# Block normalizations of the experts, keys and feed-forward stages: one fp32 product per statistic, after an addition of the two channel halves on VectorE

## What is computed

```python
def _layernorm(x, axis=-1, eps=1e-05):
    m = jnp.mean(x, axis=axis, keepdims=True)
    v = jnp.var(x, axis=axis, keepdims=True)
    return (x - m) / jnp.sqrt(v + eps)
...
h = _layernorm(x, axis=-1) * (1 + cb) + sb
x = x + gb * _L0_ffn_ref(h, L0_ffn_w_router, L0_ffn_w_gate, L0_ffn_w_down)
...
h = _layernorm(x, axis=-1) * (1 + ca) + sa
x = x + ga * _L1_attn_ref(h, L1_attn_Wq, L1_attn_Wk, L1_attn_Wphi, L1_attn_Wy_w, L1_attn_Wy_b, L1_attn_We_w, L1_attn_We_b)
...
h = _layernorm(x, axis=-1) * (1 + cb) + sb
x = x + gb * _L1_ffn_ref(h, L1_ffn_w1_w, L1_ffn_w1_s, L1_ffn_w2_w, L1_ffn_w2_s, L1_ffn_h1_w, L1_ffn_h1_s, L1_ffn_h2_w, L1_ffn_h2_s, L1_ffn_w3_w, L1_ffn_w3_s)
```

## Time and profile before

| | |
|---|---|
| median of 3 runs (lowest to highest) | 4892.88 us (4888.24 to 4893.66) |
| the profiled execution | 4881.97 us |
| its span | 4880.3 us |
| PE busy | 4384.0 us (90%) |
| DVE (VectorE) busy | 3936.3 us (81%) |
| ACT (ScalarE) busy | 3422.2 us (70%) |
| POOL (GpSimd) busy | 3121.2 us (64%) |
| stage B, from the span's start | 811 to 975 us |
| stage K | 1076 to 1193 us |
| stage R | 4167 to 4880 us |

### The profile page before, as it was taken

How to read it: one execution, slowest core, us unless ns; L and a number is a source line. 1 busy time by engine, 2 the same in 40 slices (tenths; PEclk the granted TensorE clock), 3 DMA queues, 4 the chain that set the end, 5 groups by cost and what they waited for, 6 DMA issues and landing times.

```text
span 4880.3 us, 84137 instructions
## 1 busy us (share of the span) xinstructions
PE 4384.0 (90%) x28586; PEld 2320.3 (48%) x28586; DVE 3936.3 (81%) x6598; ACT 3422.2 (70%) x2401; POOL 3121.2 (64%) x2716
## 2 busy tenths in 40 slices
PE   7888876888899999999999999999999998899998
PEld 3333333475344444444444444444444444677777
DVE  2889786625899999999999999999999999322225
ACT  2223221322999999999999999999999998444443
POOL 1576572532777777777777777777777776243334
PEclk8888777889999999999999999999999999999999
DMA  6000001353000000000000000000000001100002
GB/s 224 0 0 1 0 0 40 119 182 135 1 5 2 2 4 2 17 4 2 2 4 2 17 4 2 2 4 2 11 5 3 3 5 36 71 18 9 17 26 87
DMA packets 70909, 131.01 MB, mean 27 GB/s; under 512 B 8279, under 2 KB 46647, under 8 KB 66160
## 3 DMA queue, kind: packets, MB, share of 16 engines
q1 hardware_dynamic: 61552, 106.21, 6.4%
q0 software_dynamic: 9216, 23.17, 1.3%
HBM read 74.66 MB, written 61.03 MB: 28 GB/s over the span
## 4 chain that ended last, share of the span: by engine, by line
DVE 36%; PE 19%; issue 18%; ACT 6%; POOL 4%; DVEq 1%; POOLq 1%; DMA 0%; another core or an unknown queue 0%; ACTq 0%; SPq 0%
DVE e_slots L811 23%; PE banks L2318 11%; DVE e_slots L768 5%; ACT e_slots L599 2%; DVE ew L811 2%; POOL e_slots L695 2%; PE banks L465 1%; PE banks L1667 1%; POOL e_slots L701 1%; DVE half_max L775 1%; ACT L620 1%; ACT e_slots L590 1%; PE banks L1721 1%; ACT L603 1%; PE banks L506 1%
## 5 line engine op out<-in xcount | busy, mean ns | idle before, releaser
L811 DVE CUSTOM_DVE_ANT_0 e_slots<-e_slots,banks 128x1024 f32<-128x1024 f32 x2048 | 2389.6, 1216 | 41.6 <-PE banks L506 34.3
L599 ACT ACTIVATE e_slots<-e_slots 128x4096 f32<-128x4096 f32 x512 | 1851.8, 3624 | 89.8 <-POOL e_slots L701 65.5
L506 PE MATMUL banks<-ex_parts,sel 128*128 128x512 f32 x4096 | 1481.2, 448 | 175.1 <-DVE ew L811 127.6
L695 POOL TENSOR_SCALAR e_slots<-k,qt 128x1024 f32<-128x1024 f32 x889 | 988.3, 1121 | 587.5 <-DVE e_slots L768 509.5
L465 PE MATMUL banks<-e_slots,w_score 128*32 128x256 f32 x16384 | 1186.9, 391 | 77.4 <-ACT e_slots L599 76.2
L506 PEld LDWEIGHTS banks<-ex_parts,sel 128*128 128x128 f32 x4096 | 633.6, 189 | 894.4 <-DVE ew L811 750.4
L701 POOL TENSOR_SCALAR e_slots<-e_slots,qt 128x1024 f32<-128x1024 f32 x889 | 987.2, 1122 | 51.2 <-POOL e_slots L695 25.5
L465 PEld LDWEIGHTS banks<-e_slots,w_score 128*32 128x32 f32 x16384 | 392.6, 109 | 719.2 <-issue 401.2
L590 ACT ACTIVATE e_slots<-k,qt 128x1024 f32<-128x1024 f32 x508 | 564.6, 1135 | 1.5 <-DVE ew L811 1.4
L2448 POOL TENSOR_TENSOR g_l<-tmp,g_h 128x512 fp32r<-128x512 f32 x192 | 260.4, 1356 | 420.1 <-ACT g_h L2415 288.2
L768 DVE TENSOR_SCALAR e_slots<-k,qt 128x1024 f32<-128x1024 f32 x635 | 431.9, 748 | 0.0
(11 more groups left out here) (360 smaller groups left out, 4907.2 us busy)
## 6 DMA issues: line engine op xcount, KB each, us to landing
stage<-in_h SPq DMA_DIRECT2D x16, 1024.0 KB, 4.9
moe_slots<-empty_slot SPq DMA_DIRECT2D x1, 10320.0 KB, 38.2
slots<-moe_slots SPq DMA_DIRECT2D x8, 1290.0 KB
moe_out<-empty_slot SPq DMA_DIRECT2D x1, 8192.0 KB, 59.0
two_rows<-moe_out SPq DMA_DIRECT2D x16, 512.0 KB, 6.0
stage<-in_w SPq DMA_DIRECT2D x6, 1024.0 KB, 6.6
w_down<-in_w_down SPq DMA_DIRECT2D x1, 4096.0 KB, 12.2
x_between<-x_tokens SPq DMA_DIRECT2D x8, 512.0 KB, 3.7
```

The source lines that it names most:

```text
L506: ins = nc.tensor.matmul(spread[n % 2][:, half * W:(half + 1) * W], c_["sel"][:, half, n, :], ex_parts[:, par, :], start=True, stop=True)
L599: nc.scalar.activation(e_slots[:, par, four, :], e_slots[:, par, four, :], ACT.Sqrt, bias=EPS_RHO).then_inc(sqrt_done, 1)
L695: nc.gpsimd.tensor_scalar(e_slots[:, par, n, :], k2[:, :], FLT_MAX, qt[:, par, 1, place(n):place(n) + 1], ALU.min, ALU.max).then_inc(z_cla ...
L811: nc.vector.tensor_tensor_reduce(out=e, in0=e, in1=spread[n % 2], scale=1.0, scalar=0.0, op0=ALU.mult, op1=ALU.add, accum_out=ew[:, q, pla ...
```

## The change

In the stages B, K and R (all blocks of R but the first, whose normalization is made in stage C) VectorE adds the two channel halves of the tokens into a buffer of 128 x 512 (`b_sum`, `k_sum`, and in stage R the no longer used `empty_slot`), and the two halves of the squares in place. PE then makes one product where it made two. Two new semaphores, `halves_summed` and `squares_summed`, tell PE. The wait for the loaded tokens goes from PE's `mean` to VectorE's new `summed`, which in stage R is the first thing in VectorE's `ffn`. The stages A and C are as before.

```diff
@@ -213,7 +213,7 @@
...
                      ("taken", [P, E], fp32), ("taken_now", [P, E], fp32), ("row", [P, BT], fp32),
...
-                     ("expert", [P, E], fp32), ("out_row", [P, NTT], fp32), ("ln_even", [P, 6 * W], fp32)] + LN_BUFFERS("b2"))
+                     ("expert", [P, E], fp32), ("out_row", [P, NTT], fp32), ("b_sum", [P, 2, W], fp32), ("ln_even", [P, 6 * W], fp32)] + LN_BUFFERS("b2"))
         b_ |= phase([("slots", [P, N_SLOTS, SPP, SLOT_W], fp32), ("hid_t", [P, 3, HC, P], fp32),
...
                      ("first", [P, SPP], fp32), ("second", [P, SPP], fp32), ("w_first", [P, SPP], fp32),
@@ -225,7 +225,7 @@
                       ("cvec", [P, CC], fp32), ("cdiag", [P, CC, P], fp32), ("crow", [P, C], fp32),
                       ("k_sd", [P, W // P], fp32), ("k_rs", [P, W // P], fp32),
...
-                      ("v_out", [P, 2, W // P * C], fp32), ("k_cent", [P, 2, CC, W], fp32), ("k_sq", [P, CC, W], fp32)])
+                      ("v_out", [P, 2, W // P * C], fp32), ("k_cent", [P, 2, CC, W], fp32), ("k_sq", [P, CC, W], fp32), ("k_sum", [P, W], fp32)])
         b_base.close()
         x_layer0.close()
...
@@ -264,6 +264,7 @@
         mod_loaded, mod_tanh, mod_silu, first_mm, mod1_loaded, mod1_mm = (sem(s) for s in (
             "mod_loaded", "mod_tanh", "mod_silu", "first_mm", "mod1_loaded", "mod1_mm"))
         consts_ready = sem("consts_ready")
+        halves_summed, squares_summed = sem("halves_summed"), sem("squares_summed")
         lnm, lnc, lns, lnv, lnd, lno = (sem(s) for s in (
             "ln_mean", "ln_centered", "ln_squared", "ln_var", "ln_std_done", "ln_out"))
 
@@ -402,6 +403,7 @@
...
 
         LN_R = ln_first["R"]
+        r_sum = empty_slot[:, 0:W]
 
         N_C_LOADS = 6
 
@@ -1585,12 +1587,15 @@
             first = ln_first["B"]
 
             def mean(i):
-                ln_pe_mean(pe, first + i, x_of(i))
+                pe.wait_ge(halves_summed, i + 1)
+                pe.wait_ge(lnc, first + i + 1)
+                nc.tensor.matmul(bank(6), ones_mean[:, :], b_["b_sum"][:, i % 2, :], start=True, stop=True).then_inc(lnm, 1)
 
             def var(i):
 
                 pe.wait_ge(lnd, first + i)
-                ln_pe_var(pe, ln_b[i % 2], first + i)
+                pe.wait_ge(squares_summed, i + 1)
+                nc.tensor.matmul(bank(7), ones_mean[:, :], ln_b[i % 2][1][:, 0, :], start=True, stop=True).then_inc(lnv, 1)
 
             def router(i):
                 pe.wait_ge(lno, first + i + 2)
@@ -1691,17 +1696,17 @@
                 ins.then_inc(out_mm_b, 1)
 
             def k_mean(i):
-                pe.wait_ge(x_moe, i + 1)
-                ln_pe_mean(pe, LN_K + i, x_of(i))
+                pe.wait_ge(halves_summed, NBLK + i + 1)
+                pe.wait_ge(lnc, LN_K + i + 1)
+                nc.tensor.matmul(bank(6), ones_mean[:, :], k_ph["k_sum"][:, :], start=True, stop=True).then_inc(lnm, 1)
 
 
             def k_var(i):
-                pe.wait_ge(lns, LN_K + i + 1)
+                pe.wait_ge(squares_summed, NBLK + i + 1)
                 pe.wait_ge(lno, LN_K + i + 1)
                 for t in range(TPB):
-                    for k in range(CC):
-                        ins = nc.tensor.matmul(banks[:, 7, t:t + 1], k_ph["k_sq"][:, k, t * P:(t + 1) * P], ones_mean[:, 0:1],
-                                               start=k == 0, stop=k == CC - 1, skip_group_check=True)
+                    ins = nc.tensor.matmul(banks[:, 7, t:t + 1], k_ph["k_sq"][:, 0, t * P:(t + 1) * P], ones_mean[:, 0:1],
+                                           start=True, stop=True, skip_group_check=True)
                 ins.then_inc(lnv, 1)
 
             def spread_root(i):
@@ -1864,6 +1869,15 @@
                 dve.wait_ge(lnm, first + i + 1)
                 nc.vector.tensor_tensor(ln_b[i % 2][0][:, :, :], X[:, :, i * W:(i + 1) * W],
...
+
+            def summed(i):
+                nc.vector.tensor_tensor(b_["b_sum"][:, i % 2, :], X[:, 0, i * W:(i + 1) * W], X[:, 1, i * W:(i + 1) * W],
+                                        ALU.add).then_inc(halves_summed, 1)
+
+            def squares(i):
+                sq = ln_b[i % 2][1]
+                dve.wait_ge(lns, first + i + 1)
+                nc.vector.tensor_tensor(sq[:, 0, :], sq[:, 0, :], sq[:, 1, :], ALU.add).then_inc(squares_summed, 1)
 
             def normed(i):
                 b = i // BPB
@@ -1947,18 +1961,26 @@
...
                 nc.vector.tensor_copy(b_["slot_of"][:, b, :, :], packed[:, 3:5, :]).then_inc(rows_ready, 1)
 
+            summed(0)
+            summed(1)
             centred(0)
             centred(1)
+            squares(0)
+            squares(1)
+            summed(2)
             normed(0)
             normed(1)
             logits(0)
             dve.wait_ge(lno, first + 1 + 1)
             centred(2)
             logits(1)
+            squares(2)
             less_max(1)
             dve.wait_ge(cum_read, 1)
             choose(0)
             for i in range(NBLK):
+                if i + 3 < NBLK:
+                    summed(i + 3)
                 if i + 2 < NBLK:
                     normed(i + 2)
                 if i:
@@ -1970,6 +1992,8 @@
                 if i % BPB == 0:
                     place_rows(i // BPB)
                 silu(i, 1)
+                if i + 3 < NBLK:
+                    squares(i + 3)
                 if i + 2 < NBLK:
                     logits(i + 2)
                     if (i + 2) % BPB == BPB - 1:
@@ -2020,6 +2044,16 @@
...
                                                          x, ALU.mult, ALU.add)
                 ins.then_inc(x_moe, 1)
+                dve.wait_ge(x_moe, i + 1)
+                if i:
+                    dve.wait_ge(lnm, LN_K + i)
+                nc.vector.tensor_tensor(k_ph["k_sum"][:, :], X[:, 0, i * W:(i + 1) * W], X[:, 1, i * W:(i + 1) * W],
+                                        ALU.add).then_inc(halves_summed, 1)
+
+            def k_squared(i):
+                sq = k_ph["k_sq"]
+                dve.wait_ge(lns, LN_K + i + 1)
+                nc.vector.tensor_tensor(sq[:, 0, :], sq[:, 0, :], sq[:, 1, :], ALU.add).then_inc(squares_summed, 1)
 
             def k_centred(i):
                 dve.wait_ge(lnm, LN_K + i + 1)
@@ -2106,6 +2140,7 @@
             add(0)
             k_centred(0)
             add(1)
+            k_squared(0)
             k_rooted(0)
             k_centred(1)
             k_normed(0)
@@ -2113,6 +2148,8 @@
                 queries(i)
                 if i == NBLK - 1:
                     row_masks()
+                if i + 1 < NBLK:
+                    k_squared(i + 1)
                 if i + 2 < NBLK:
                     add(i + 2)
                 if i + 1 < NBLK:
@@ -2306,7 +2343,6 @@
             end_phase(sp, ph["R"])
 
         def pe_r(pe):
-            bufs = [w_["r_cent"], w_["r_sq"], w_["r_std"], w_["r_std"]]
...
 
             def product(dst, w, o, hi, lo, n_k, ready=None):
@@ -2321,8 +2357,13 @@
 
             def mean(b, h):
                 n = ln_first_r(b * BPB + h)
-                pe.wait_ge(xr_loaded[h], b * 16 + 16)
-                ln_pe_mean(pe, n, w_["xr"][:, h, :, :])
+                pe.wait_ge(halves_summed, b * BPB + (2 * NBLK + h))
+                pe.wait_ge(lnc, n + 1)
+                nc.tensor.matmul(bank(6), ones_mean[:, :], r_sum, start=True, stop=True).then_inc(lnm, 1)
+
+            def var(b, h):
+                pe.wait_ge(squares_summed, b * BPB + (2 * NBLK + h))
+                nc.tensor.matmul(bank(7), ones_mean[:, :], w_["r_sq"][:, 0, :], start=True, stop=True).then_inc(lnv, 1)
 
             def ffn(b, h, nxt):
                 i = b * BPB + h
@@ -2346,7 +2387,7 @@
                         pe.wait_ge(hi_done, i * PARTS + (OC + o - 1))
...
                 if nxt:
-                    ln_pe_var(pe, bufs, ln_first_r(nxt[0] * BPB + nxt[1]))
+                    var(*nxt)
                 pe.wait_ge(stage_free, H2_CAST)
                 for o in range(OC):
                     pe.wait_ge(hi_done, i * PARTS + (2 * OC + o - 1))
@@ -2469,6 +2510,9 @@
                 dve.wait_ge(xr_loaded[h], b * 16 + 16)
...
                                         ALU.subtract).then_inc(lnc, 1)
+                sq = w_["r_sq"]
+                dve.wait_ge(lns, n + 1)
+                nc.vector.tensor_tensor(sq[:, 0, :], sq[:, 0, :], sq[:, 1, :], ALU.add).then_inc(squares_summed, 1)
                 dve.wait_ge(lnd, n + 1)
                 own.link(nc.vector.reciprocal(std[:, :], std[:, :]))
                 own.link(nc.vector.tensor_tensor(cent[:, :, :], cent[:, :, :],
@@ -2487,9 +2531,15 @@
                 own.link(nc.vector.tensor_reduce(w_["bad"][:, c:c + 1], t, AX, ALU.add))
                 dve.sem_inc(stage_free if c < NW - 1 else w_checked, 1)
 
+            def summed(b, h):
+                dve.wait_ge(xr_loaded[h], b * 16 + 16)
+                nc.vector.tensor_tensor(r_sum, x[:, h, 0, :], x[:, h, 1, :], ALU.add).then_inc(halves_summed, 1)
+
```

(2 more changed lines are left out.)

## The result

The changed kernel takes **4935.66 us** (4935.06 to 4939.65, 4 runs) where the kernel before, measured beside it, takes 4890.56 (4887.27 to 4893.66): ratio **1.0096**, 95% interval 1.0084 to 1.0109, so 41 to 53 us slower. The forecast was 4936, in a range of 4911 to 4956.

What follows compares the result with a forecast made beforehand. PE was taken to bound stages K and R nearly throughout, PE and VectorE stage B; VectorE gates R's block heads. R +42.7, K -2, B +3 on the profiled 4881.97 gave 4925.7, or 4936 against the runs' median; range 4911 to 4956.

Steps and rivals of the forecast that it cites:

- The place: Head of stage R blocks: the addition and its load wait come ahead of VectorE's first gated operation, in six blocks.
- The stall, 6.9 us: Stage R: VectorE's first gated operation begins 6.9 us late in six blocks, +41.5 us.
- The clock, +1.6 a stall: Stage R: PE at 1.2 GHz for some 3.3 us of work after each of six stalls, +9.6 us in all.
- the rival of the colder clock: Stage R: third and fourth gated parts both slow after a stall, +6.6 us, 4943; chance 0.10.
- The savings in R, -8.4: Stage R: shorter products save 7 x 0.86 = 6.0 us on variances and 6 x 0.4 = 2.4 on means.
- Stage K, -2: Stage K: net 2 us shorter, with ends -5 (additions free) and +3 (root uncovered, clock late).
- so 0.1 is gained, times 7: Stage K blocks: variance halves to 0.84 us, but its squares come 0.7 us after PE would start.
- Stage B, +3: Stage B: net 3 us longer; ends -10 (PE decides everywhere) and +9 (all additions show, PE cools).
- The sum: Whole kernel: R 42.7, K -2, B +3 give +43.7 us; forecast 4936 against the runs' median.
- Full clock: Rival, stage R: load wait as forecast, but PE isn't throttled by the stalls; 4926, chance 0.08.
- The load in time: Rival, stage R: load lands before VectorE's first gated operation, only products shrink; 4885.5 or 4872, chance 0.04.
- B or K pays more: Rival: VectorE bounds stage B and uncovers the root in K, 6 + 5 us more, 4947; chance 0.08.

Runs made afterwards that it cites:

- r_sum_mid: The changed kernel with stage R's addition of the next block's halves moved from ahead of the first gated part to ahead of the fifth; ratio 1.0001 to the kernel before.

## Why the prediction was right, and where it wasn't

- **The place.** Right, by its own step: VectorE's first operation of a block waits for `xr<-x_before_ffn`, six times, and both gated operations queue behind it. The wait alone reproduces the loss. Each of those blocks is 8.1 us longer (forecast some 7.5).
- **The stall, 6.9 us.** Measured 6.98, x6 = 41.9. It's the step that came closest, because each of its terms (SP's 3.11, which is the store's way to landing, 3.1 us in the median; the load's landing; the addition) had a row. The addition, assumed 0.67, took 0.69. The load took 4.2 us. The fit in the Trainium skill, "DMA: Bandwidth & Descriptors", section "Anatomy of one DMA — SWDGE (gpsimd) path", would give 3.2 as an estimate for 512 KB. That section is about DMAs issued from GpSimd and these are issued by SP, which the prediction didn't say; the store's 3.1 agrees with the estimate and the load's 4.2 doesn't.
- **The clock, +1.6 a stall.** Mis-sized. "The fourth is mostly fast again" failed: 1.2 GHz lasted for some 6 us of work and not 3.3, so third and fourth parts are both slow. Measured 6.55 less 4.39 = 2.2 in the first block; on average over the six 6.21 less 4.45 = 1.8 to the fifth part's start, and 14.83 less 12.68 = 2.15 to the next block's mean: +13 in all and not +9.6. "The fifth waits for the third" failed too: in the changed kernel's first stalled block it's the sixth that waits. The upper end, 2.7, held it, and so the rival of the colder clock was half right.
- **The savings in R, -8.4.** Measured -7.4 with the stall taken away (704.2 against 711.6). The mis-sized term is the mean's: from mean to variance a block goes from 30.73 to 30.53 us, so 0.2 is gained and not 0.4, since PE waits 0.25 to 0.32 us for POOL next. With the variance's 6.0 that makes 7.2. Sum of R: 41.9 + 13 - 7.4 = 47.5; the stage shows 47.2 (prediction 42.7).
- **Stage K, -2.** Wrong in sign: +4.3, beyond the end of +3. The failed step is "so 0.1 is gained, times 7". A looped block loses 0.15 instead, as its variance starts 0.94 us later and not 0.7; and the last block has other neighbours on PE, so that its 1.65 us of wait and the half clock behind it (the values' product 2.60 us for 1.97, the transposes 1.91 for 1.05) were in no row I had read. The root stayed hidden, as said. The start of the stage gave nothing back: from POOL's first addition to the first keys it takes 21.1 us on average in six changed traces and 21.0 in five old ones, as PE stands 2.83 us for the squares there.
- **Stage B, +3.** 3.2 in the pair of the result, 6 to 7 in the sets; within its ends. The reason was not "VectorE's reciprocals and choices mostly decide" alone: PE waits for both additions, as the prediction feared of the mean, and the lower clock kept most of what the products gave, which it had in the upper end only. This account is read from the traces and not tested by a run.
- **The sum.** +43.7 forecast; between the profiled executions it is +53.7, 10 more, of which 4.7 are R's (47.4 less 42.7), 3.8 K's (6.3 by the means of the traces) and 1.9 stage C's, where nothing was changed. The predicted 4936 met the median because the sum was set on the runs' 4892.88 and the changed kernel's own profile had no such offset (4935.71 against 4935.66). The mechanism and the size were right; that they agree to the last 10 us is two errors that cancel.
- **The rivals.** Full clock: out. The load in time: out. B or K pays more: this one also came true, in K.

## What to carry to other kernels

A wait costs what stands behind it on its engine, in program order: here 52 us of loss hang on a line that computes nothing, and four gated parts further down the same addition is free. After a stall of PE, price the clock too (2.2 us behind a stall of 7); and in a stage where PE has little idle time, count on it that shorter products with new waits in between may lose in clock what they save in work (stage B: 2.7 us less busy time for 13.8 of shorter products). Before halving a product, ask stage by stage whether it's on the chain; and price first and last blocks by their own rows, since their neighbours differ.

## What the hardware showed that was not expected

**Additions meet POOL.** VectorE's 128x512 addition of two SBUF operands takes 0.68 to 0.69 us alone. When a POOL addition is under way it ends 0.55 us after that one ends, whatever its start (0.54 to 0.56 in all 52 such meetings of stages K and R in the traces here):

```profile
4289.23 1.02 DVE L2536 TENSOR_TENSOR empty_slot<-xr 128x512 f32<-128x512 f32 x1
```

```profile
4288.41 1.30 POOL L2489 TENSOR_TENSOR g_l<-tmp,g_h 128x512 fp32r<-128x512 f32 x1 [0.54 <-ACT g_h L2434]
```

(r_sum_mid: 4290.25 against 4289.71.) The other way round, where VectorE's addition begins 0.01 to 0.03 us ahead of POOL's at the start of stage K, it keeps its 0.69, and POOL's takes 2.87 to 2.88 us instead of some 2.36 (nine traces). VectorE's operations with an operand in PSUM keep 0.69 and 0.75 beside the same POOL work. The Trainium skill, "SBUF — State Buffer", section "SBUF: two separate sides", says of the pair of ports that both engines share that it is an exclusive lock, contended for by a VectorE operation with two SBUF inputs when the GpSimd operation reads SBUF, and that the later one waits for the whole instruction. The traces agree in both directions: the later one is the one that grows, here to 0.55 us behind the other's end. In the changed kernel this played hardly a part: its additions have medians of 683 to 693 ns, and the longest is 910.

**Less work on PE, at a lower clock.** In stage B, 1.00 became 0.83 over 40 us while PE's busy time fell from 37.96 to 35.93 us; over the whole stage 0.89 became 0.84 while it fell from 217.96 to 215.28. So most of what the products gave was lost in the speed of the rest. The shorter products and the new waits came together, and which of them did it stays open.
